# A graph network on one core: one-hot matrices moved to the scalar engine, and a node update as a wave

## The chip, the cores and the metric

The kernel runs on one core of a Trainium2 chip. The metric is the device time of one execution in microseconds (us). The core has five engines with queues of their own, which wait for each other through semaphores: TensorE (PE in the profile; its weight loads PEld), VectorE (DVE), the scalar engine (ACT), GpSimd (POOL), and SyncE (SP), which only issues transfers (DMAs).

## The reference, cut to what matters

Four graph layers run one after another on 6250 nodes with 16 features and 206250 edges sorted by destination. Nothing in the computation is changed; what follows is what the passes of the kernel compute.

```
A0, N0  m = silu(einsum(x[col], edge_attr_8, W_msg_tp)) @ W_msg_lin ; agg = segment_sum(m)
        u = silu(einsum(x, agg, W_upd_tp)) @ W_upd_lin ; x = norm(x + u)
1 to 6  six graph convolutions: h @ W, times dinv, segment sums over the edges
7       sums of x[src] * edge_weight with a running maximum over each destination's segment
        (and, beside it, relu(edge_attr_13 @ f1 + b), stored for 8 and 9)
8, 9    message e = reshape(edge_net(e), 16 x 16) @ h[src e] ; segment sum ; GRU step
```

Passes 7, 8 and 9 each go over all edges, gather a row of 16 numbers per edge, and add a result per edge into its destination's column.

## The kernel before, in words

Edges stand in 1632 tiles of 128 (one edge per partition); a batch is HT = 8 tiles, and there are NB = 204 batches, in a hardware loop of 51 turns with SL = 4 batches each. Every counter of a pass is a semaphore with a fixed number of steps per batch (`VPER` for VectorE, `TPER` for TensorE, `APER` for the scalar engine), and `at(k, step)` is its value when that step of batch k is done. h = k mod 2 picks one of two buffers.

**Cells (GpSimd, during A0 and after).** GpSimd scatters one cell per edge into the adjacency table `adj` with indirect DMAs (L591), eight per batch, and copies pairs out of `acc` (L582) ahead of each batch. It is behind A0 and ends later than A0 does. Passes 1 to 6 read `adj` in blocks (L533), and their first load waits for all cells.

**N0.** After A0 the node update runs over 13 chunks of 512 nodes, one chunk after the other, 25 steps each, each step waiting for the one before on another engine (L749 to L764 on TensorE). Its steps write `stage`, `tst`, `acc` and `arena`. `acc` still holds the pairs that GpSimd copies, so from the seventh chunk on VectorE waits for the last copy. The block loads of pass 1 wait for N0's last step. The later updates N1 to N5 are already waves: four chunks (SETS) are in flight, each with its own banks and semaphore, and the engines walk an order of (chunk, step) written out by `wave`.

**Passes 7 to 9.** GpSimd gathers: eight indirect DMAs per batch (L562), each 128 rows by indices in SBUF (`idx`), into one of four buffers `G`. It waits once per two batches, for VectorE to be done (step `USED`) with the batches that had these buffers, and for the indices. VectorE, per batch:

- loads eight destination starts into registers (`load_firsts`, L1207, L1208), and makes the one-hot (L1199): for 8 tiles, iota of 128 against `rel`, the edge's place within its tile's window, in bf16;
- subtracts for the lowest bf16 piece of the last batch's message (`lower`, L1224); a message is split in three bf16 pieces, the first two copied by the scalar engine (high L1177 or L1157, middle L1179 or L1164);
- waits for the gather and makes the message: in pass 7 L1666, then L1669, L1671 and a scan (L1676); in passes 8 and 9 four multiplies (L1711) of TensorE's products (L916, from `rT`) by the gathered rows, and a reduction (L1716);
- adds eight windows into `acc` at the registers' columns (L1215), and takes the remainder after the high piece (`remains`, L1229).

TensorE multiplies the pieces by the one-hot (`windows`, L625, eight products of a batch) once the lower piece is there. In pass 8 and 9 it does so for batch k - 1 behind the products of batch k. SyncE loads `rT` for a batch two batches on, when the remainder is taken (L484).

## Time and profile before

| | |
|---|---|
| median of 3 runs | 12295.55 us (12293.52 to 12299.69) |
| the profiled execution | 12296.19 us |
| its span, first to last instruction | 12294.4 us |
| mean granted TensorE clock | 0.667 of full speed |
| busy: TensorE, VectorE, scalar engine, GpSimd | 74%, 65%, 16%, 57% |

The stages in the span: set-up and A0 to 2630 us, N0 to 3140, passes 1 to 6 with their updates to 5430, pass 7 to 7800, pass 8 to 10030, pass 9 to the end. The profile names each group of instructions by line, engine, operation and tiles (out<-in), with the time it was busy and the idle time of its engine just before it, which is put down to what came last ("issue" where nothing that the profile shows was waited for). The windows view gives for a stretch of the span its length, the busy us and number of instructions of PE, PEld, DVE, ACT and POOL, and then the granted clock as a share of 2.4 GHz, the DMA share and GB/s.

### The profile page before, as it was taken

The numbers are of one execution on the slowest core, as the hardware profiler recorded it, in microseconds if no ns is written. First come the engines' busy times: TensorE is split into PE (matmuls) and PEld (weight loads), VectorE is DVE, ScalarE is ACT, GpSimd is POOL, SyncE is SP. The second block draws the span as 40 slices with busy tenths as digits, with TensorE's granted clock in tenths as the row PEclk, the third lists the DMA queues.
The fourth block names the chain that finished last, engine by engine and source line by source line (L and its number), as shares of the span: only waits on it lengthen the run. The fifth ranks groups of instructions, "written<-read, shape, count | busy, mean of one in ns | idle before, by whom it ended". The sixth has DMA issues, their size and how long they took to land.

```text
span 12294.4 us, 191432 instructions
## 1 busy us (share of the span) xinstructions
PE 9044.8 (74%) x51270; PEld 6037.7 (49%) x51270; DVE 7967.3 (65%) x14983; ACT 1906.5 (16%) x6193; POOL 7005.9 (57%) x6789
## 2 busy tenths in 40 slices
PE   0499999974578998756666666677777767777776
PEld 0366666641367787532222222355555545555554
DVE  1599999962122222237777777688888868888887
ACT  2454333321000100001111111000000000000000
POOL 0588788873000000027777777577777757777775
PEclk9999999975578898755555555555555555555555
DMA  7633444310887887861111111111111111111111
GB/s 253 213 104 104 118 107 109 108 50 0 258 261 242 261 287 237 278 205 33 34 34 34 34 33 34 26 19 19 19 19 19 19 20 19 19 19 19 19 19 20
DMA packets 1340598, 1146.05 MB, mean 93 GB/s; under 512 B 329039, under 2 KB 1225504, under 8 KB 1340190
## 3 DMA queue, kind: packets, MB, share of 16 engines
q1 hardware_dynamic: 1108690, 1064.47, 28.4%
q0 software_dynamic: 210560, 44.35, 4.8%
q10 hardware_dynamic: 21186, 34.95, 0.9%
q8 instruction: 116, 1.90, 0.1%
q14 instruction: 46, 0.38, 0.0%
HBM read 994.01 MB, written 144.62 MB: 93 GB/s over the span
## 4 chain that ended last, share of the span: by engine, by line
DVE 34%; PE 16%; issue 10%; DMA 7%; DVEq 7%; POOL 1%; ACT 1%; SPq 0%; POOLq 0%; ACTq 0%
DVE acc L1215 10%; DVE arena L1711 8%; DVE msg L1716 7%; DMA arena<-adj 7%; PE ps L797 7%; DVE arena L1676 4%; PE ps L876 3%; DVEq L1207 2%; PE ps L809 2%; DVEq L1215 2%; PE ps L625 2%; DVE threes L1224 1%; DVE sc L1229 1%; DVEq L1208 1%; POOL arena L562 1%
## 5 line engine op out<-in xcount | busy, mean ns | idle before, releaser
L562 POOL DMA_INDIRECT arena<-tab,idx x4896 | 4984.4, 1018 | 4315.2 <-DMA idx<-in_src_p 2619.6
L916 PE MATMUL ps<-w_w2b,arena 33*128 33x256 f32 x6528 | 2931.4, 640 | 39.7 <-DMA arena<-rT 21.9
L916 PEld LDWEIGHTS ps<-w_w2b,arena 33*128 33x128 f32 x6528 | 2106.9, 330 | 652.4 <-issue 119.0
L591 POOL DMA_INDIRECT adj<-pairs x1632 | 1865.1, 1143 | 488.1 <-issue 417.6
L625 PE MATMUL ps<-arena,threes 128*48 128x128 bf16 x4912 | 625.2, 308 | 1680.8 <-DVE threes L1224 1680.8
L1215 DVE TENSOR_TENSOR acc<-acc,ps 48x128 f32 x4920 | 1377.9, 280 | 652.5 <-PE ps L625 3.9
L625 PEld LDWEIGHTS ps<-arena,threes 128*48 128x48 bf16 x4912 | 486.9, 151 | 2287.6 <-issue 2287.6
L797 PE MATMUL ps<-arena 128*128 128x192 bf16 (+1 forms) x18816 | 1374.1, 235 | 297.7 <-DMA arena<-adj 288.6
L797 PEld LDWEIGHTS ps<-arena 128*128 128x128 bf16 x18816 | 1290.0, 104 | 394.2 <-issue 389.0
L1711 DVE TENSOR_TENSOR arena<-ps,arena 128x512 f32<-128x512 f32 x1632 | 1010.7, 681 | 26.5 <-DMA arena<-tab,idx 26.5
L1716 DVE TENSOR_REDUCE msg<-arena 128x128 f32<-128x2048 f32 x408 | 932.7, 2286 | 14.1
L994 ACT ACTIVATE wide<-ps,not_all 128x128 bf16<-128x128 f32 x1632 | 572.8, 377 | 1238.7 <-PE ps L693 1238.5
L1199 DVE TENSOR_TENSOR arena<-w_iota,rel 128x1024 bf16<-128x1024 f32 x408 | 500.9, 1228 | 385.6 <-PE ps L916 265.1
L1378 DVE TENSOR_TENSOR arena<-hot_a,threes 128x1024 bf16<-128x1024 bf16 x612 | 745.8, 1219 | 0.0
L1526 DVE TENSOR_REDUCE wide<-ps 128x128 f32<-128x384 f32 (+1 forms) x192 | 79.0, 453 | 986.3 <-PE ps L797 986.3
L1676 DVE TENSOR_TENSOR_SCAN arena<-arena,carry,ps 16x1024 f32<-16x1024 f32 x204 | 476.1, 2334 | 215.4 <-PE ps L876 215.4
L1177 ACT ACTIVATE threes<-msg 128x128 bf16<-128x128 f32 x408 | 126.2, 309 | 2832.8 <-DVE msg L1716 2826.0
L687 PE MATMUL ps<-arena 128*128 128x128 f32 x3264 | 402.7, 277 | 186.8 <-DMA arena<-tab 174.1
L1507 DVE TENSOR_TENSOR acc<-acc,ps 64x128 f32 (+1 forms) x408 | 113.7, 279 | 614.1 <-PE ps L774 572.8
L687 PEld LDWEIGHTS ps<-arena 128*128 128x128 f32 x3264 | 396.3, 194 | 201.7 <-DVEq L1372 174.7
L729 PE MATMUL ps<-acc,arena 128*128 128x392 bf16 x2448 | 422.6, 329 | 0.0
L887 PEld LDWEIGHTS ps<-w_ident,arena 16*128 16x128 f32 x1632 | 171.2, 195 | 504.8 <-issue 504.8
(241 smaller groups left out, 10059.7 us busy)
## 6 DMA issues: line engine op xcount, KB each, us to landing
arena<-adj SPq DMA_DIRECT2D x672, 896.0 KB, 7.9
arena<-rels SPq DMA_DIRECT2D x204, 512.0 KB
arena<-tab SPq DMA_DIRECT2D x1632, 64.0 KB
adj<-zero SPq DMA_DIRECT2D x49, 2048.0 KB, 20.7
arena<-tab,idx POOLq DMA_INDIRECT x4896, 2.4
arena<-rT SPq DMA_DIRECT2D x408, 128.0 KB
adj<-pairs POOLq DMA_INDIRECT x1632
rT<-spare ACTq DMA_DIRECT2D x204, 128.0 KB
```

The costliest lines, as they stand in the source:

```text
L562: pool.indirect_dma_start(G[b][:, u, 0:FEAT[PHASES[p]]], None, TABLE[PHASES[p]], bass.IndirectOffsetOnAxis(ap=idx[b // 2][:, b % 2 * HT + ...
L591: pool.indirect_dma_start(adj_cells, bass.IndirectOffsetOnAxis(ap=pairs[h][:, u, 0:1], axis=0), pairs16[h][:, u, 2:3], None).then_inc(cell ...
L625: last = mm(ps[0:48, 2 * h + u // 4, (u % 4) * P:(u % 4 + 1) * P], threes[h][:, u, :, :].rearrange("p k f -> p (k f)"), hot[h][:, u, :], s ...
L687: last = mm(ps[:, 2 + 2 * h + u // 4, (u % 4) * P:(u % 4 + 1) * P], hotT[h][:, u * P:(u + 1) * P], nodes0[h][:, u, :], start=True, stop=True)
L797: last = mm(ps[:, 2 * par + u // 2, u % 2 * W:(u % 2 + 1) * W], ring[i][:, s, u * P:(u + 1) * P], rows[:, j * SC + s, :, :].rearrange("p k ...
L916: last = mm(ps[:, 4 + q, (u % 2) * 256:(u % 2 + 1) * 256], row[h][0:33, u * P:(u + 1) * P], w["w2b"][:, :], start=True, stop=True)
L994: act_fn(junk[u % 2], ps[:, 6 + u // 4, (u % 4) * P:(u % 4 + 1) * P], ACT.Relu, bias=not_all[:, :], accum_out=equals[h][:, u:u + 1]).then_ ...
L1215: tt(dst[0:F, ds(v, P)], dst[0:F, ds(v, P)], window(u), ALU.add).then_inc(vec[p].sem, 1)
L1378: tt(placed[h][:, i, :, :, :], hot_a[:, :, :].unsqueeze(3).to_broadcast([P, HT, A8, 16]), threes[h][:, :, i, :].unsqueeze(2).to_broadcast( ...
L1676: nc.vector.tensor_tensor_scan(wk[0:16, HE:], wk[0:16, 0:HE], ps[0:16, 4:6, :].rearrange("p q n -> p (q n)"), carry[:, 0:1], ALU.add, ALU. ...
L1711: tt(wk[:, q * 512:(q + 1) * 512].rearrange("p (u o i) -> p u o i", u=2, i=16), ps[:, 4 + q, :].rearrange("p (u o i) -> p u o i", u=2, i=1 ...
L1716: nc.vector.tensor_reduce(msg[h][:, :, :].rearrange("p u o -> p (u o)"), wk[:, :].rearrange("p (x i) -> p x i", i=16), AX, ALU.add).then_i ...
```

## The change

Two parts.

In passes 7, 8 and 9 VectorE no longer makes one-hots. The scalar engine does, a batch ahead: after the middle piece of batch k it writes, for each of 8 tiles of batch k + 1, the square of (rel - iota) into `far2` (Square with scale -1 and a bias per partition), and then Relu(1 - 2 x square) of all 1024 columns into `hot`, after TensorE's windows that last read this buffer. `rel` and `rel_last` are padded by a batch, since the last turn makes a one-hot that nobody reads. TensorE's windows wait for the scalar engine's count too. VectorE's step numbers go down by one. Its register load is behind L1671 in pass 7; in passes 8 and 9 it is done for two batches at a time, 16 registers, in every even batch.

N0 becomes a wave like N1 to N5, of 26 steps, four chunks in flight, with buffers of their own in `arena` (`a_0` to `t_0`), the 256-row product in two halves, and no copies of x. The column of `acc` that each chunk kept is no longer written by a step: two multiplies of x and dinv after the wave do it, the first for columns 0 to 3263, the second, after all cells have landed, for the rest. The block loads of pass 1 wait for the cells and the wave. At the start, two memsets become one and two are new.

```diff
+        far2 = arena[:, 7 * HE:8 * HE].rearrange("p (u n) -> p u n", u=HT)
...
-        K = dict(A0=3, N0=25)
-        WAVES = dict(N1=11, N2=12, N3=21, N4=12, N5=11)
+        K = dict(A0=3)
+        WAVES = dict(N0=26, N1=11, N2=12, N3=21, N4=12, N5=11)
...
-        USED = [None] + [None] * 6 + [3, 6, 6]
-
-        VPER = [18] + [7] * 6 + [8 + HT] * 3
+        USED = [None] + [None] * 6 + [2, 5, 5]
+
+        VPER = [18] + [7] * 6 + [7 + HT] * 3
         TPER = [2 + HT] + [NCH + 1] * 6 + [5, 5, 5]
-        APER = [3 + HT, 1, 1, 1, 1, 1, 1, 4, 2, 2]
+        APER = [3 + HT, 1, 1, 1, 1, 1, 1, 6, 4, 4]
         LOADS = [0, 0, 0, 0, 0, 0, 0, 4, 1, 1]
...
-        LOWER = 2
-        MSG, CHANGED, RESET, SCAN, CARRY = range(3, 8)
-        MUL = [3, 4, 5, 6]
-        MESSAGES = 7
-        END0 = 8
+        LOWER = 1
+        MSG, CHANGED, RESET, SCAN, CARRY = range(2, 7)
+        MUL = [2, 3, 4, 5]
+        MESSAGES = 6
+        END0 = 7
         REMAINS = END0 + HT
         WT = [1, 2, 3, 4]
         WINDOWS8 = 5
...
                 if p == 1:
-                    before = node[PHASES[p]]
-                    sp.wait_ge(before.sem, before.at(NC - 1, before.per))
+                    nodes_done(sp, 1)
...
             def windows(p, k, h):
 
+                pe.wait_ge(scl[p].sem, scl[p].at(k - 1, APER[p]))
                 pe.wait_ge(vec[p].sem, vec[p].at(k + 1, LOWER))
...
+            for c, step in wave("N0"):
+                i, x = c % SETS, xT[:, c * CH:(c + 1) * CH]
+                if step == 1:
+                    wave_wait(pe, "N0", c, 1)
+                    for a8 in range(A8):
+                        last = mm(ps[0:16, 2 * i, :].rearrange("p (b a) -> p a b", a=A8)[:, a8, :],
+                                  lin8[:, a8 * 16:(a8 + 1) * 16], agg[:, c * (CH // A8):(c + 1) * (CH // A8)],
+                                  start=True, stop=True)
+                    last.then_inc(wave_sem[i], 1)
+                elif step in (3, 6):
+                    wave_wait(pe, "N0", c, step)
+                    half = slice(0, P) if step == 3 else slice(P, 2 * P)
+                    mm(ps[:, 2 * i, :], w["rep_i"][:, half], x, start=True, stop=True)
+                    mm(ps[:, 2 * i + 1, :], w["rep_h"][:, half], a_0[i][0:16, :], start=True, stop=True
+                       ).then_inc(wave_sem[i], 1)
+                elif step == 9:
+                    wave_wait(pe, "N0", c, 9)
+                    mm(ps[0:16, 2 * i, :], w["upd_tp"][:, 0:16], x_0[i], start=True, stop=False)
+                    mm(ps[0:16, 2 * i, :], w["upd_tp"][:, 16:32], y_0[i], start=False, stop=True).then_inc(wave_sem[i], 1)
+                elif step == 11:
...
+            for c, step in wave("N0"):
+                i = c % SETS
+                if step in (2, 4, 7, 10, 18, 23, 25):
+                    wave_wait(act, "N0", c, step)
+                low, high = ps[:, 2 * i, :], ps[:, 2 * i + 1, :]
+                p_w, rows = piece(16)[:, c * 4:c * 4 + 4, :, :], low[:, 0:64].rearrange("p (j f) -> p j f", j=4)
+                if step == 2:
+                    act_fn(a_0[i][0:16, :], low[0:16, :], ACT.Copy, scale=0.25).then_inc(wave_sem[i], 1)
+                elif step == 4:
+                    act_fn(x_0[i], low, ACT.Copy).then_inc(wave_sem[i], 1)
...
-            open_pass(act, scl[7], 7)
+            def squares(p, k, h, r):
+
+                for u in range(HT):
+                    last = act_fn(far2[:, u, :], w["iota"][:, :], ACT.Square, scale=-1.0, bias=r[:, ds(k * HT + u, 1)])
+                last.then_inc(scl[p].sem, 1)
+
+            def one_hot(p, k, h):
+
+                act.wait_ge(scl[p].sem, scl[p].at(k - 1, APER[p] - 1))
+                act_fn(hot[h][:, :, :], far2[:, :, :], ACT.Relu, scale=-2.0, bias=unit[:, :]).then_inc(scl[p].sem, 1)
+
+            def open_one_hots(p, r):
+
+                stage_done(act, PHASES[p])
+                act.sem_inc(scl[p].sem, SL * APER[p] - 2)
+                squares(p, 0, 0, r)
+                one_hot(p, 0, 0)
+
+            open_one_hots(7, rel_last)
...
+                    act.wait_ge(scl[7].sem, scl[7].at(k - 1, APER[7]))
+                    squares(7, k + 1, 1 - h, rel_last)
+                    act.wait_ge(ten[7].sem, ten[7].at(k - 1, WINDOWS7))
+                    one_hot(7, k + 1, 1 - h)
...
+                        act.wait_ge(scl[p].sem, scl[p].at(k - 1, APER[p]))
+                        squares(p, k + 1, 1 - h, rel)
+                        act.wait_ge(ten[p].sem, ten[p].at(k, WINDOWS8))
+                        one_hot(p, k + 1, 1 - h)
...
-            def one_hot(p, k, h, r):
-
-                dve.wait_ge(ten[p].sem, ten[p].at(k - 2, TPER[p]))
-                tt(hot[h][:, :, :], w["iota"][:, :].unsqueeze(1).to_broadcast([P, HT, P]),
-                   r[:, ds(k * HT, HT)].unsqueeze(2).to_broadcast([P, HT, P]), ALU.is_equal
-                   ).then_inc(vec[p].sem, 1)
-
-            first_node = [dve.alloc_register(f"first_node{u}") for u in range(HT)]
-
-            def load_firsts(k):
-
-                dve.load(first_node, base[0:1, ds(k * HT + HT, HT)])
-                return [dve.snap(r, min_val=0, max_val=N) for r in first_node]
+            first_node = [dve.alloc_register(f"first_node{u}") for u in range(2 * HT)]
+
+            def load_firsts(k, n=HT):
+
+                dve.load(first_node[0:n], base[0:1, ds(k * HT + HT, n)])
+                return [dve.snap(r, min_val=0, max_val=N) for r in first_node[0:n]]
...
-            with dve.Fori(0, 2 * T // CH) as c:
-                update_nodes(c)
-            dve.wait_ge(pairs_in, NB)
-            with dve.Fori(2 * T // CH, NC) as c:
-                update_nodes(c)
+            for c, step in wave("N0"):
+                i, x = c % SETS, xT[:, c * CH:(c + 1) * CH]
+                if step in (5, 8, 12, 13, 15, 16, 19, 20, 21, 24, 26):
...
+                if step == 5:
+                    tt(x_0[i], x_0[i], high, ALU.mult).then_inc(wave_sem[i], 1)
+                elif step == 8:
+                    tt(y_0[i], y_0[i], high, ALU.mult).then_inc(wave_sem[i], 1)
...
+            nodes_done(dve, 1)
+            tt(acc[0:16, 0:2 * T], xT[:, 0:2 * T], dinv[0:16, 0:2 * T], ALU.mult).then_inc(sums_open, 1)
+            for h in range(2):
+                dve.wait_ge(celled[h], 16 * HT * NB // 2)
+            tt(acc[0:16, 2 * T:], xT[:, 2 * T:], dinv[0:16, 2 * T:], ALU.mult).then_inc(sums_open, 1)
+            dve.wait_ge(sums_open, 2)
...
-                    at = load_firsts(k - 1)
-                    one_hot(7, k, h, rel_last)
                     lower(7, k - 1, 1 - h)
...
 
+                    at = load_firsts(k - 1)
                     dve.wait_ge(v.sem, v.at(k, RESET))
...
-                        at = load_firsts(k - 1)
-                        one_hot(p, k, h, rel)
+                        if h == 0:
+                            at = load_firsts(k - 1, 2 * HT)
                         lower(p, k - 1, 1 - h)
```

## Rows read from the trace of the kernel before

**Rows 1.** The page, parts 1, 4 and 5: totals, chain by line, costly groups.
```profile
PE 9044.8 (74%) x51270; PEld 6037.7 (49%) x51270; DVE 7967.3 (65%) x14983; ACT 1906.5 (16%) x6193; POOL 7005.9 (57%) x6789
...
DVE acc L1215 10%; DVE arena L1711 8%; DVE msg L1716 7%; DMA arena<-adj 7%; PE ps L797 7%; DVE arena L1676 4%; PE ps L876 3%; DVEq L1207 2%; PE ps L809 2%; DVEq L1215 2%; PE ps L625 2%; DVE threes L1224 1%; DVE sc L1229 1%; DVEq L1208 1%; POOL arena L562 1%
...
L1716 DVE TENSOR_REDUCE msg<-arena 128x128 f32<-128x2048 f32 x408 | 932.7, 2286 | 14.1
```

**Rows 2.** One line's instructions, passes 7, 8, 9: ns min/median/max, first and last start.
```profile
L1666 DVE TENSOR_TENSOR msg<-arena,col x204: 278/286/293, 5451.7 to 7780.5; 128x128 f32<-128x128 f32 x102
...
L1711 DVE TENSOR_TENSOR arena<-ps,arena x816: 673/681/692, 7850.8 to 10003.9; 128x512 f32<-128x512 f32 x164
...
L1711 DVE TENSOR_TENSOR arena<-ps,arena x816: 679/681/692, 10078.6 to 12224.0; 128x512 f32<-128x512 f32 x164
```

**Rows 3.** The gathers of pass 9: durations, starts, idle time before them, landing.
```profile
L562 POOL DMA_INDIRECT arena<-tab,idx x1632: 940/944/1920, 10067.3 to 12217.8; - x182
...
  issue: 497.1, 1631
...
DMA to landing us min/median/max: 2.1/2.4/3.6
```

**Rows 4.** Windows of N0, of the N3 wave and of pass 9.
```profile
2631.00:3140.00 509.00, 234.09 (x494) 69.04 (x494) 129.44 (x158) 93.17 (x117) 221.28 (x250) 0.52 0.01 0
4224.00:4347.00 123.00, 104.95 (x156) 15.79 (x156) 63.72 (x116) 51.44 (x91) 0.00 (x0) 0.51 0.09 29
10200.00:12140.00 1940.00, 1498.12 (x4410) 1093.70 (x4410) 1570.49 (x2942) 113.52 (x367) 1492.02 (x1471) 0.50 0.13 19
```

**Rows 5.** Timeline of pass 8, one batch's turn: start us, duration us, engine, line.
```profile
9014.17 0.28 DVE L1229 TENSOR_TENSOR sc<-msg,threes 128x128 f32<-128x128 f32 x1
9014.48 0.31 ACT L1179 ACTIVATE threes<-sc 128x128 bf16<-128x128 f32 x1 [3.09 <-DVE sc L1229]
9014.62 0.32 SPq L484 DMA_DIRECT2D arena<-rT  x1
...
9015.21 1.22 DVE L1199 TENSOR_TENSOR arena<-w_iota,rel 128x1024 bf16<-128x1024 f32 x1 [0.76 <-PE ps L916]
9015.91 1.34 POOL L562 DMA_INDIRECT arena<-tab,idx  x1 [0.30 <-issue]
9016.35 0.28 DVE L1224 TENSOR_TENSOR threes<-sc,threes 128x128 bf16<-128x128 f32 x1
9016.55 1.28 DVE L1711 TENSOR_TENSOR arena<-ps,arena 128x512 f32<-128x512 f32 x2
...
9016.78 1.02 PE L625 MATMUL ps<-arena,threes 128*48 128x128 bf16 x8 [2.25 <-DVE threes L1224]
```

**Rows 6.** Register loads on VectorE's queue, passes 8 and 9.
```profile
L1207 DVEq TENSOR_LOAD <-base x402: 593/598/811, 7901.4 to 12198.9; - x134
```

**Rows 7.** Groups of the scalar engine in N0: busy us, mean ns.
```profile
L958 ACT ACT_TABLE_LOAD x39 | 50.0, 1283 | 1.2
...
L958 ACT ACTIVATE arena<-ps 128x1024 f32<-128x1024 f32 x13 | 13.3, 1023 | 170.1 <-PE ps L755 170.1
```

**Rows 8.** Timeline of pass 7, VectorE alone.
```profile
6515.10 0.28 DVE L1229 TENSOR_TENSOR sc<-ps,threes 128x128 f32<-128x128 f32 x1
...
6517.28 0.29 DVE L1224 TENSOR_TENSOR threes<-sc,threes 128x128 bf16<-128x128 f32 x1
6517.48 0.28 DVE L1666 TENSOR_TENSOR msg<-arena,col 128x128 f32<-128x128 f32 x1
6517.69 1.21 DVE L1669 TENSOR_TENSOR arena<-arena 16x1024 f32<-16x1024 int32 x1
```

**Rows 9.** Timeline: end of the scatters, first block load, first product of pass 1.
```profile
2918.13 0.95 POOL L591 DMA_INDIRECT adj<-pairs  x1 [0.30 <-issue]
...
3140.17 26.20 SPq L533 DMA_DIRECT2D arena<-adj  x10
...
3146.55 1.28 PE L797 MATMUL ps<-arena 128*128 128x48 bf16 x28 [5.94 <-DMA arena<-adj]
```

More of the change, by code:

```diff
@@ L743, in _, with product @@
             mm(ps[:, 7, 0:Q // P], first[:, :], node_q[:, :], start=True, stop=True).then_inc(positions, 1)
[L744 removed]
+            def product(name, c, step, F, out, lhsT, rhs):
+                wave_wait(pe, name, c, step)
+                mm(ps[0:F, 2 * (c % SETS) + out, :], lhsT, rhs, start=True, stop=True).then_inc(wave_sem[c % SETS], 1)
             pe.wait_ge(agg_in, 2)
[L746 to L764 removed]
@@ new lines, in _ @@
+            for c, step in wave("N0"):
[18 more added lines that the diff above has]
+                elif step == 11:
+                    product("N0", c, 11, 16, 1, w["upd_lin"][:, :], b_0[i][0:16, :])
+                elif step == 14:
+                    product("N0", c, 14, 16, 0, w["mean16"][:, :], b_0[i][0:16, :])
+                elif step == 17:
+                    product("N0", c, 17, 16, 1, w["mean16"][:, :], a_0[i][0:16, :])
+                elif step == 22:
+                    wave_wait(pe, "N0", c, 22)
+                    for j in range(4):
+                        last = nc.tensor.transpose(ps[:, 2 * i, j * 16:(j + 1) * 16], g_0[i][0:16, j * P:(j + 1) * P],
+                                                   w["ident"][0:16, 0:16])
+                    last.then_inc(wave_sem[i], 1)
@@ L805, in sum_pass @@
                     ten[p + 1].open(pe)
-            def product(name, c, step, F, out, lhsT, rhs):
-                wave_wait(pe, name, c, step)
-                mm(ps[0:F, 2 * (c % SETS) + out, :], lhsT, rhs, start=True, stop=True).then_inc(wave_sem[c % SETS], 1)
             def wave_rows(name, c, step, F, out):
@@ L1170, in _ @@
             for p in (8, 9):
[L1171 removed]
+                open_one_hots(p, rel)
                 with act.Fori(0, IT) as it:
@@ L1283, in split_rest @@
                    ).then_inc(n.sem, 1)
-            for half in range(2):
-                nc.vector.memset(zero[:, half * CH // 2:(half + 1) * CH // 2], 0.0).then_inc(ready, 1)
+            nc.vector.memset(zero[:, :], 0.0).then_inc(ready, 1)
+            nc.vector.memset(rel_last[:, T:], 0.0).then_inc(ready, 1)
             nc.vector.memset(lin8[:, :], 0.0).then_inc(ready, 1)
@@ L1720, in _ @@
                         dve.wait_ge(ten[p].sem, ten[p].at(k, WINDOWS8))
-                        add_windows(p, k, at, acc, 48, END0, range(HT), half_window(1 - h, 48))
+                        add_windows(p, k, at[h * HT:(h + 1) * HT], acc, 48, END0, range(HT), half_window(1 - h, 48))
                         remains(p, k, h, msg[h][:, :, :])
```

96 lines of the change are left out of this document (46 added, 50 removed).

## The prediction

> **What bounds the kernel now.** I read the engine totals and the chain first. VectorE is busy 65% of the span, GpSimd 57%, and the chain is led by VectorE's adds, multiplies and reductions [rows 1]. That suggests a kernel bound by VectorE, where each instruction taken off it is time won. The views by pass say otherwise.
>
> The last three passes have 204 batches each. In pass 9, VectorE's first multiply starts at 10078.6 and its last, the fourth of its batch (three times some 0.6 behind the first), at 12224.0: (12222.2 - 10078.6) / 203 = 10.56 us a batch; in pass 8 it is 10.60, in pass 7 11.47 [rows 2]. Now GpSimd: 1632 gathers in pass 9, median 0.944 us, and the idle time before them, 497.1 us in 1631 gaps, is put down to nothing but issue: 0.305 each [rows 3]. In a stretch of that pass GpSimd's mean is 1492.02 / 1471 = 1.014 [rows 4], and 8 x (1.014 + 0.305) = 10.55: a whole batch. GpSimd never waits; both engines fill the batch.
>
> The timeline of one batch shows what couples them [rows 5]. The one-hot (L1199) runs 9015.21 to 9016.43. The gather that starts inside it, at 9015.91, takes 1.34 instead of 0.94 and ends at 9017.25, 0.82 after the one-hot. A median gather ends 0.82 after a point 0.13 from its start, so I read: a gather reads its indices there and is held until the one-hot ends. Multiplies (one input in PSUM) hold none. GpSimd's own pace is 8 x (0.944 + 0.305) = 9.99 us a batch; the rest is the one-hot's hold, once a batch.
>
> **One-hots to the scalar engine (VectorE side).** Call R the start of the remainder (L1229). Today: R at 9014.17, register load, one-hot at 9015.21, lower piece (L1224) at 9016.35, multiply at 9016.55, so 2.38 from R [rows 5]. The load (0.6 [rows 6], and what uses it) fills the 1.04 before the one-hot. Without one-hot the lower piece waits for the scalar copy of the middle piece (L1179, 9014.48 to 9014.79, hidden today): it starts at R + 0.66 and the multiply at R + 0.86. Every second batch of passes 8 and 9 still loads registers there, 16 now: no row has 16, bounds are one load's 0.6 and two loads' 1.2; I take 0.9, lower piece at R + 1.3. VectorE's batch becomes 10.60 - 2.38 + 0.86 = 9.1, or 9.7: mean 9.4; with the dear load 9.55.
>
> **The gathers' side.** 9.99 is above 9.4, so GpSimd sets passes 8 and 9, and of the 1.2 us that VectorE loses only 0.6 is won. The last batch's first multiply comes 203 x 9.99 = 2028 after the first batch's. Pass 8: 7850.8 + 2028 = 9878.8 against 10003.9 - 1.8 = 10002.1: 123.3. Pass 9: 12106.6 against 12222.2: 115.6. Sum 238.9 [rows 2, 3]; the lower piece (two inputs in SBUF, 0.28) may hold a few gathers, so 235, range 200 to 240.
>
> [...]
>
> **Scalar engine.** Added per batch: eight squares of 128x128 and a Relu of 128x1024. The nearest rows are L1179's 0.31 (128x128) and 1.02 (L958, 128x1024) [rows 5, 7]: 8 x 0.31 + 1.02 = 3.5. As upper bound I double the square, since each takes its bias from a computed address: 6.0. They start after the middle copy, R + 0.62, and end at R + 4.1 (6.6). Queued behind is the next high copy, possible at R + 0.86 + 2.5 + 2.3 = R + 5.7 [rows 1, 5], needed only by the next remainder three microseconds on. At 3.5 nothing is late, at 6.0 the slack takes it. TensorE reads a one-hot a batch later. If Square is not in the loaded table, two loads of 1.28 [rows 7] are added: 6.1, hidden too. [...]
>
> **TensorE** is busy 1498.12 in 1940 us, 8.2 a batch [rows 4]. It fits 9.99. Its rT load, issued at R + 0.45 (9014.62 [rows 5]), would be needed 1.5 earlier than today; 2.4 us of landing, the gathers' own [rows 3], gives R + 2.8; with the 7.2 of products (8.2 less the windows' 1.0 [rows 5]) they end at R + 10.0, and the last multiply wants them at R + 0.86 + 1.9 + 9.99: hidden.
>
> **Pass 7.** R to lower piece is 2.18 today (6515.10 to 6517.28) [rows 8]. It becomes 0.74 (the scalar copy stands behind a Relu there); from the lower piece on, TensorE's windows and transposes set the scan as now; the register load moves under L1671. VectorE: 11.47 - 1.44 = 10.0. GpSimd: 9.99 plus the hold of L1669, which stays: two SBUF inputs, 1.21 us, nearly the 1.25 between two gathers' starts, so some gather nearly always meets it. Once VectorE follows the landing, its place is fixed: with E the end of the eighth gather and D its landing time, L1669, 0.21 behind the message multiply [rows 8], runs from E + D + 0.26 to E + D + 1.47; gathers read at E + 1.68 and E + 2.93. D of 1.45 to 1.68 costs 0 to 0.2, D of 1.9 costs 0.4, D below 1.42 a full 1.2. Landing from start is 2.4 [rows 3] (D 1.4 to 1.5), longer when SyncE's four loads go out at the same time, as they would here; I take D = 1.9: 10.4 a batch, (11.47 - 10.4) x 203 = 217. Bounds: 10.05 (288) and 11.18 (59).
>
> **N0.** Today the last scatter of cells starts at 2918.13 (landed about 2920.3); the first block load is issued at 3140.17, and the first product of pass 1 is at 3146.55 [rows 9]. As a wave, N0 is bound by TensorE: 234.1 us of products [rows 4]. The N3 wave kept TensorE busy 104.95 of 123 us at a granted clock of 0.51 [rows 4], 85%: 234.1 / 0.85 = 275, so N0 ends at 2906, under the scatters, which then gate the loads: first product at 2920.3 + 6.4 = 2926.7, 220 earlier. The two new multiplies into acc (3264 and 3392 columns; at L1711's 0.64 for 512 [rows 5], 4.2 each) run before and within those 6.4. If the clock rose the wave would be shorter and nothing gained. Two-input instructions may hold scatters: 216. At 70% it ends at 2965 and 173 is left.
>
> **Sum.** 216 + 217 + 235 = 668 off the profiled 12296.2 (span 12294.4; median of the runs 12295.55, the same): 11628.
>
> **Rivals.**
> A. VectorE alone sets the pace, as the chain says: (10.6 - 9.4) x 408 = 490, pass 7 298, N0 216: 11292. Against it: gathers cannot go below 9.99. Chance 0.05.
> B. Gathers are not freed: another cause makes them 1.014 in the mean. Passes 8 and 9 stay near 10.55 and win nothing; pass 7 at about 10.8 wins 136, N0 216: 11944. Against it: each long gather overlaps a one-hot. 0.08.
> C. Pass 7 settles in the full hold, 11.18: 11786. 0.12.
> D. Slower: a scalar batch longer than today's 10.6, from (10.6 - 1.6) / 8 = 1.1 us a square (small instructions with an address and bias from registers could be dear). At 1.3, 12.0 a batch: 408 x 1.45 + 203 x 1.9 - 216 = 761 slower, 13057. Against it: 0.31 in each such row. 0.03, with 0.01 of it near no change.
> My forecast has 0.72.
>
> **Range.** Best bounds: 220 + 288 + 240 = 748, 11548. C with nothing else is 11786. 11540 to 11800 leaves out A, B, D and a bit of C with a late wave. A change within 0.2% (25 us) can't be told from none: faster 0.97, same 0.01, slower 0.02.
>
> **What would show it.** Passes 8 and 9: gather mean back at 0.944 to 0.95, no gather over 1.3, the multiply released by the landing, batch 9.99. Pass 7: gathers still over 1.0 beside L1669, message multiply waiting for the gather. N0: last step before 2930, first block load at 2920 to 2925. Wrong if the gathers stay long, if the multiply waits for TensorE or the lower piece for the scalar engine past R + 1, or if the wave passes 2960.

## The result, and the profile after

| | before | after |
|---|---|---|
| median time, us | 12297.62 (4 runs, 12293.52 to 12306.68) | 11517.97 (4 runs, 11513.64 to 11525.68) |
| profiled execution, us | 12296.19 | 11525.68 |

The ratio is 0.9366, 95% interval 0.935 to 0.9382: 780 us saved, where 668 were forecast, and a time 22 us below the low end of the range. The direction was right, and so were the mechanisms of the three terms; the sum lacked a fourth term.

Page of the changed kernel, parts 1, 4 and 5 (against [rows 1]):

```profile
PE 8973.8 (78%) x51270; PEld 6020.0 (52%) x51270; DVE 7298.7 (63%) x14361; ACT 4035.9 (35%) x11725; POOL 6700.9 (58%) x6789
...
POOL arena L569 31%; PE ps L820 8%; DMA arena<-adj 5%; DVE msg L1779 3%; PE ps L754 2%; DVE arena L1774 2%; DMA arena<-tab,idx 2%; PE ps L935 2%; DVE acc L1266 1%; PE ps L797 1%; PE ps L633 1%; ACT x_all L1106 0%; SPq L455 0%; DMA arena<-rT 0%; DVE x_all L1606 0%
...
L1184 ACT ACTIVATE arena<-w_iota,rel 128x128 f32<-128x128 f32 x3280 | 998.1, 386 | 0.2
...
L1190 ACT ACTIVATE arena<-arena,unit 128x1024 bf16<-128x1024 f32 x615 | 706.0, 1148 | 20.0
```

The chain, led by VectorE's adds, multiplies and reductions before, is now led by GpSimd's gathers (L569, 31%). The views by line say the same of passes 8 and 9. First the multiply of both passes and what its engine waited for, in the kernel before:

```profile
L1711 DVE TENSOR_TENSOR arena<-ps,arena x1632: 673/681/692, 7850.8 to 12224.0; 128x512 f32<-128x512 f32 x182
...
  DMA arena<-tab,idx: 26.5, 2
```

The same after the change, pass by pass, and then the gathers of pass 9 (against [rows 2, 3]):

```profile
L1774 DVE TENSOR_TENSOR arena<-ps,arena x816: 673/680/693, 7317.5 to 9349.3; 128x512 f32<-128x512 f32 x164
...
L1774 DVE TENSOR_TENSOR arena<-ps,arena x816: 673/680/693, 9423.2 to 11453.1; 128x512 f32<-128x512 f32 x164
...
  DMA arena<-tab,idx: 186.6, 219
```

```profile
L569 POOL DMA_INDIRECT arena<-tab,idx x1632: 940/944/1063, 9412.0 to 11448.0; - x182
its engine sat idle before it (us, times) until:
  issue: 481.8, 1581
...
DMA to landing us min/median/max: 2.2/2.4/3.3
```

The longest gather of pass 9 is 1.06 us (1.92 before). A batch of pass 8 is (9349.3 - 1.8 - 7317.5) / 203 = 10.00 us, of pass 9 9.99, forecast 9.99. In 219 of the 408 batches VectorE's multiply now waits for the landing of a gather, 0.46 us a batch in the mean; before, it did so twice, once at the start of each pass.

N0's end, and the first products of pass 1 (timeline; against [rows 9]):

```profile
2928.69 0.95 POOL L598 DMA_INDIRECT adj<-pairs  x1 [0.30 <-issue]
...
2931.06 3.68 DVE L1556 TENSOR_TENSOR acc<-x_all,dinv 16x3392 f32<-16x3392 f32 x1 [45.43 <-DMA adj<-pairs]
2931.37 17.52 SPq L540 DMA_DIRECT2D arena<-adj  x8
...
2936.94 1.28 PE L820 MATMUL ps<-arena 128*128 128x48 bf16 x28 [1.64 <-DMA arena<-adj]
```

The wave was done early: VectorE had waited 45 us for the scatters before the second of its two multiplies. The last scatter starts 10.6 us later than before, the first product 209.6 earlier.

One line remains, the one that the prediction never asked for: the products of the six passes with sums, in the kernel before and after, from the first of pass 1 to the last of pass 6.

```profile
L797 PE MATMUL ps<-arena x18816: 182/246/368, 3146.6 to 5396.9; 128*128 128x192 bf16 x132, 128*128 128x48 bf16 x67
```

```profile
L820 PE MATMUL ps<-arena x18816: 182/246/368, 2936.9 to 5109.9; 128*128 128x192 bf16 x132, 128*128 128x48 bf16 x67
```

2250.3 us became 2173.0, though no instruction of these passes was changed. The spans' difference of 770.5 us is made up so (the 0.2 us that the rows lack are rounding and the step from the last product to the first gather):

| stretch | saved, us | forecast |
|---|---|---|
| up to the first product of pass 1 | 209.6 | 216 |
| passes 1 to 6 and their updates | 77.3 | none |
| first gather of pass 7 (5440.3; 5153.2) to first multiply of pass 8 | 246.2 | 217 |
| from there to the end | 237.2 | 235 |

### The profile page after: what moved, and what is told of

It is laid out like the page before. It is cut to its first block, busy times and chain, and to the rows that moved or that the text cites. A ratio compares the mean times of both kernels' runs of the same rounds, so it can differ in the third digit from the quotient of the medians.

```text
span 11523.9 us, 201355 instructions
## 1 busy us (share of the span) xinstructions
PE 8973.8 (78%) x51270; PEld 6020.0 (52%) x51270; DVE 7298.7 (63%) x14361; ACT 4035.9 (35%) x11725; POOL 6700.9 (58%) x6789
## 4 chain that ended last, share of the span: by engine, by line
POOL 31%; PE 14%; issue 12%; DMA 8%; DVE 7%; DVEq 1%; ACT 1%; SPq 1%; POOLq 0%; ACTq 0%
POOL arena L569 31%; PE ps L820 8%; DMA arena<-adj 5%; DVE msg L1779 3%; PE ps L754 2%; DVE arena L1774 2%; DMA arena<-tab,idx 2%; PE ps L935 2%; DVE acc L1266 1%; PE ps L797 1%; PE ps L633 1%; ACT x_all L1106 0%; SPq L455 0%; DMA arena<-rT 0%; DVE x_all L1606 0%
## 5 line engine op out<-in xcount | busy, mean ns | idle before, releaser
L569 POOL DMA_INDIRECT arena<-tab,idx x4896 | 4675.6, 955 | 3843.8 <-DMA idx<-in_src_p 2290.4
L820 PE MATMUL ps<-arena 128*128 128x192 bf16 (+1 forms) x18816 | 1341.5, 234 | 229.9 <-DMA arena<-adj 214.4
L1184 ACT ACTIVATE arena<-w_iota,rel 128x128 f32<-128x128 f32 x3280 | 998.1, 386 | 0.2
L1190 ACT ACTIVATE arena<-arena,unit 128x1024 bf16<-128x1024 f32 x615 | 706.0, 1148 | 20.0
L1233 ACT ACTIVATE threes<-sc 128x128 bf16<-128x128 f32 x408 | 126.2, 309 | 1295.3 <-DVE sc L1280 1295.3
L1275 DVE TENSOR_TENSOR threes<-sc,threes 128x128 bf16<-128x128 f32 x615 | 181.7, 295 | 588.1 <-issue 334.8
```

The costliest lines, as they stand in the source:

```text
L569: pool.indirect_dma_start(G[b][:, u, 0:FEAT[PHASES[p]]], None, TABLE[PHASES[p]], bass.IndirectOffsetOnAxis(ap=idx[b // 2][:, b % 2 * HT + ...
L820: last = mm(ps[:, 2 * par + u // 2, u % 2 * W:(u % 2 + 1) * W], ring[i][:, s, u * P:(u + 1) * P], rows[:, j * SC + s, :, :].rearrange("p k ...
L1184: last = act_fn(far2[:, u, :], w["iota"][:, :], ACT.Square, scale=-1.0, bias=r[:, ds(k * HT + u, 1)])
L1190: act_fn(hot[h][:, :, :], far2[:, :, :], ACT.Relu, scale=-2.0, bias=unit[:, :]).then_inc(scl[p].sem, 1)
```

## Experiments

Two things must be known to read them. First, of 18 runs only three (chunks_half, chunks_fit, arena_128), all on one chip, were made where the kernel before takes its 12297 us. On the four other chips it took 14771 to 15108. There single register instructions of VectorE, SyncE and, after the change, the scalar engine take up to 1.4 us instead of 0.05, and the work behind them starts later; I call this late streams. The register instruction ahead of each add, in the kernel before where it takes 12297 us:

```profile
L1215 DVEq FUSED_REGOPS  x4920: 46/46/46, 5456.7 to 12235.2; - x197
```

and with late streams, in the kernel before with a pad, with what the adds waited for:

```profile
L1216 DVEq FUSED_REGOPS  x4920: 1/46/1423, 6066.5 to 14946.6; - x197
...
its engine sat idle before it (us, times) until:
  issue: 745.7, 408
```

That "issue" is time in which the adds waited for nothing that the profile shows; in the kernel before without late streams they have none of it. So the times of passes 7 to 9 say little about the change there. Passes 1 to 6 hardly depend on it: the changed kernel's 2173.0 us was 2176.2 with late streams, and 2170.3 to 2183.5 in the four runs that edit passes 7 to 9 alone (mults_sbuf, its two repeats, no_compare). Differences under some 10 us are therefore not read. Second, the measure for passes 1 to 6 is always the one above, first to last product.

### The arena's place

The change adds tiles ahead of the arena, which receives the block loads in packets of 1024 bytes: eight columns to rel_last, and unit, 36 bytes per partition as declared. The arena's place is named below by the declared bytes that stand ahead of it and don't in the kernel before: 0 there, 36 after the change. The address at which it then begins stands in no trace; where an expectation counts a move otherwise (64 for the change's tiles in hots_part, 128 in arena_128), that is the expectation's own count, which no run shows.

```diff
+        pad = sb("pad", [P, 9])     # before_pad36; [P, 7] in after_pad28, [P, 1] in before_pad4
         eps = sb("eps", [P, 1])
```

> The kernel before with one unused tile of 36 bytes per partition ahead of eps and of the arena; no instruction changes. Passes 1 to 6, which the prediction took as unchanged, gave back about 77 us of the change's 780 (the profiled executions: 2293.8 us from the first product of pass 1 to the first gather before, 2216.3 after). Theory A (the change moved the arena by 36 bytes per partition, and the 1024-byte packets of the block loads then take 46 ns instead of 46 to 60): the packets take 46 ns here too, passes 1, 3, 4 and 6 become about 19, 8, 8 and 19 us shorter and passes 2 and 5 about 12, and the run is about 78 us faster, near 12220. Theory B (the loops of the passes stand elsewhere in the instruction stream, and other loops have to be fetched over and over): nothing moves here, 12297 within 0.2%, and passes 2 and 5 stay the long ones of the middle four.

Measured: ratio 0.9939 (0.9917 to 0.9961), 15008 against 15098 us; first to last product 3861.9 to 6006.8, 2144.9 us: 105 shorter than before by an unused tile, where 78 were expected. Theory A holds.

> The changed kernel with one unused tile of 28 bytes per partition, so that the arena stands 64 bytes behind its place in the kernel before, at the same remainder by 64. Theory A (the arena's place sets the packets' time): the 1024-byte packets of the block loads go back to 46 to 60 ns, and about 78 us of the 780 are lost: 11596. Theory B (the place of the loops in the instruction stream): 11518 within 0.2%.

Measured: 0.9821 (0.9801 to 0.984) and 2270.8 us, 98 longer than the changed kernel. With 64 declared bytes ahead of it the arena is at a slow place again. The control is the changed kernel as it is:

> The changed kernel as it is, as the control of the two that follow, and against its version with 28 more bytes per partition, which gave 0.9821 of the kernel before. If the arena's place is worth the same 0.6% here, this one gives about 0.976 on a chip like that of the first four runs, and 0.937 on one like that of the kernel's own runs.

Measured: 0.9799 (0.9774 to 0.9824), 2176.2 us. The stretch shows A; the intervals of the two ratios overlap, and they come from two chips.

> The kernel before with one unused tile of 4 bytes per partition ahead of eps, instead of the 36 of the first pad; no instruction changes. The 36 bytes took about 90 us off. [...]

Measured: ratio 1.0 (0.9985 to 1.0015), 2254.0 us. Four bytes do nothing (2250.3 without them); the pad of 36 gave 2144.9.

> The changed kernel with three small tiles moved from behind the arena to ahead of it and one of 4 bytes added, so that the arena begins 128 bytes later per partition. [...]

Measured, with 12299 for the kernel before: 11606.37 us (11599.45 to 11610.59), 0.9436, and 2257.3 us. The four tiles declare 16 bytes, 52 with the change's 36: a slow place. This is the one run that shows the arena's place in the time of the whole kernel: 88 us over the changed kernel's 11518, with intervals of the ratios that don't meet. The packets themselves, DMA view of 2960 to 3020 in this kernel and in the changed one:

```profile
GB/s 350 348 348 349 350 350 351 349 348 349 350 346 349 348 350 348 349 348 348 350 348 347 355 343 350 348 350 357 339 349 348 348 349 350 348 347 355 335 331 276
```

```profile
GB/s 386 388 384 380 380 385 388 384 386 387 384 378 384 385 386 379 386 386 386 377 384 385 386 359 383 386 385 387 386 386 386 389 353 359 280 83 1 11 68 251
```

With its queues full, the core moves 349 GB/s into one arena and 386 into the other. By packet: in every run with the arena at 36, 97 to 98% take 46 or 47 ns; at the four other places, 0, 4, 52 and 64, 37 to 40% do, and the mean is 51. The fast place was one in all runs, and what sets it apart from the other four wasn't shown.

### The place of the loops

Within passes 1 to 6 some got longer. Of the kernel before, passes 2 and 3, and of the changed one, passes 2 and 3 again (the products; then, from the DMA view of each pass, the queue of instruction fetches: packets, MB, share). Before:

```profile
L797 PE MATMUL ps<-arena x3136: 242/246/364, 3517.6 to 3841.9; 128*128 128x192 bf16 x196
...
L797 PE MATMUL ps<-arena x3136: 242/246/364, 3922.9 to 4219.3; 128*128 128x192 bf16 x196
```

```profile
q8 instruction: 35, 0.57, 0.6%
...
q8 instruction: 7, 0.11, 0.1%
```

After:

```profile
L820 PE MATMUL ps<-arena x3132: 242/246/368, 3289.6 to 3579.0; 128*128 128x192 bf16 x196
...
L820 PE MATMUL ps<-arena x3136: 242/246/368, 3660.0 to 3973.3; 128*128 128x192 bf16 x196
```

```profile
q8 instruction: 7, 0.11, 0.2%
...
q8 instruction: 35, 0.57, 0.5%
```

324.3 and 296.4 us became 289.4 (290.0 with the first four products, which the window leaves out) and 313.3, and the fetches changed sides with the time (a window holds one or two fetches more than its pass). The traces also show the size of a fetch in instructions. A packet is 16384 bytes; in the passes 2 to 5 that got six of them, before and after, TensorE's stream had 256 to 265 instruction records from one to the next in the mean, and a round of the loop has 1696 (6783 in the four). And they show where a loop begins beside the fetches: in the passes 2 to 5 with six fetches, in these two kernels, a fetch came 89 to 104 records ahead of the first product; in those with 34 none came in the 40 us ahead of it, and the first came 10 to 37 records behind it. So TensorE's stream got fillers:

```diff
+                for _ in range(FILL[p]):      # half: 120 for p = 1; fit: 36, 34, 16, 118 for p = 1, 3, 4, 5
+                    pe.sem_inc(filler, 1)
                 nodes_done(pe, p)
```

> The changed kernel with 120 increments of an unused semaphore on TensorE's queue ahead of pass 1. TensorE's instruction stream is read in packets of 16 KB, 256 instructions of 64 bytes; the loop of one of the passes 1 to 6 is 1700 instructions, 6.64 packets. Counted in the compiled streams, the loops that begin in the first third of a packet (passes 3, 4 and 6 before; 2 and 5 after the change) are those whose trace has 6 such packets, and those that begin later (2 and 5 before; 1, 3 and 4 after) have 33 and last 22 to 26 us longer. Theory B1 (a loop that lies in 8 packets is read again in every round, one in 7 is not): the 120 put the loops back where the kernel before has them: pass 1 falls from 295 to about 273 us (the run with 36 bytes), 3 and 4 from 308 to 282, 6 from 271 to 263, passes 2 and 5 rise from 283 to about 307; the sum from 1746 to about 1715, 30 us off the changed kernel. Theory B2 (the fetches only go with long passes, something else sets them): the pattern stays, long passes 1, 3 and 4, and the time within 0.2%.

Measured: 11496.57 us (11495.05 to 11500.42), 0.9349 (0.9337 to 0.9362); passes 272, 312, 287, 289, 316 and 263 us (counted from first to last product of each, which is 1 to 5 more than the count in the expectation), 2147.6 in all against 2173.0. The fetches changed sides with the loops, and 120 instructions that do nothing made this stretch 25 us shorter: B1 holds. In the whole kernel that is 0.2%, and there the ratio's interval still meets that of the changed kernel (0.935 to 0.9382).

> The changed kernel with 36, 34, 16 and 118 such increments ahead of passes 1, 3, 4 and 5, so that every one of the six loops begins in the first third of a packet of 16 KB of TensorE's stream. Theory B1: no pass is read again, six fetches each; passes 1 to 6 at about 273, 282, 282, 282, 282 and 263 us, 1664 instead of 1746: 80 us less, 0.5 to 0.7% off the changed kernel and the fastest version so far. Theory B2: no change, or the increments' own time of 5 to 10 us more.

Measured: 11488.05 us (11483.96 to 11491.57), 0.9342 (0.9329 to 0.9355), 30 off instead of 80; first to last product 2134.8 us. Passes 1, 3, 4 and 6 as expected, 3, 4 and 5 with a fetch 4 to 17 records ahead of their first product. Two misses: pass 2 was read again (34 fetches, 314 us), with its first fetch 169 records behind its first product and none just ahead; and the 118 increments ahead of pass 5 stand bare, 18 us in which TensorE does nothing:

```profile
4465.41 0.80 PE L814 MATMUL ps<-arena,zero 128*128 128x384 bf16 x2 [18.02 <-issue]
```

The next version spreads them over the groups of the update ahead, where TensorE waits anyway:

```diff
+            first_step = dict(N1=2, N2=2, N3=4, N4=2, N5=4)
             def product(name, c, step, F, out, lhsT, rhs):
+                if step == first_step.get(name):
+                    fill(FILL[int(name[1])] * (c + 1) // NC - FILL[int(name[1])] * c // NC)
                 wave_wait(pe, name, c, step)
```

> The changed kernel with all six loops of passes 1 to 6 in the first quarter of a 16 KB packet of TensorE's stream (the sixth at 0.34, where it had 6 fetches in the last version): 100 increments ahead of pass 1, and 106, 122, 16 and 118 spread over the groups of the updates N1 to N4, each just ahead of a product for which TensorE waits anyway (an increment took 0.15 us; 8 or 9 of them against a wait of 1.1 to 1.4 us). Theory B1: six fetches in every pass; the passes at about 266, 282, 282, 281, 282 and 263 us, 1656 instead of 1744, with up to 10 us lost again in the updates: 11518 - 78 = 11440. If pass 2 is still read again, the place within the packet isn't the rule.

Measured, with 14773 for the kernel before: 14409.16 us, 0.9751 (0.9726 to 0.9777), 80 us below the changed kernel's 14488.97, which was measured where the kernel before took the same time (14771). First to last product 2102.0, and no pass is read again; in passes 2 to 5 a fetch came 32 to 53 records ahead of the first product. Once more:

> The version with all six loops early in a packet, once more. In its first run every pass had 6 fetches and passes 1 to 6 took 272, 284, 284, 285, 285 and 264 us, 1674 in sum (1746 for the changed kernel on such a chip), and the kernel 0.9751 of the one before against 0.9799 for the changed kernel. Where no engine's stream is late (the kernel before at 12297): 11518 - 70 + up to 10 for the increments = 11448 to 11458. On the other kind of chip: 0.975 again.

Measured: late streams again (15108 for the kernel before), 0.9717 (0.969 to 0.9743; 0.975 was expected), 2105.3 us. Its pass 2, 289.9 us with 6 fetches:

```profile
L832 PE MATMUL ps<-arena x3136: 242/246/364, 3995.4 to 4285.3; 128*128 128x192 bf16 x196
```

```profile
q8 instruction: 6, 0.10, 0.1%
```

It is the fastest version by these stretches; its time where the kernel before takes 12297 wasn't measured.

### The two parts by themselves

n0_part applies the lines on N0 alone, hots_part the rest.

> The kernel before with N0's wave alone; arena, one-hots and registers as before. Up to the first product of pass 1 the profiled executions differ by 210 us. Theory A (arena's place, which stays here): 12297 - 210 = 12087. Theory B (the unrolled wave moves the loops of passes 1 to 6 in the instruction stream): 12297 - 210 - 77 = 12010, with passes 3 and 4 the long ones of the middle four, as in the changed kernel. A mixture: the long passes change places, but the sum of passes 1 to 6 stays at 2294 us.

> The kernel before with the part on passes 7 to 9 alone: one-hots on the scalar engine a batch ahead, registers for two batches, and the tiles that they bring (so the arena is moved by 36 bytes here too); N0 stays the loop of 25 steps. The time after N0 accounts for 246 (pass 7) and 238 (passes 8 and 9) of the saving in the profiled executions. Theory A (arena's place) adds the 77 of passes 1 to 6: 12297 - 484 - 77 = 11736. Theory B (place in the instruction stream, which the unrolled wave of N0 moves): 12297 - 484 = 11813, and passes 2 and 5 stay the long ones of the middle four, as before.

Measured: 0.9885 (0.9865 to 0.9904) with 2273.2 us, and 0.9872 (0.9852 to 0.9892) with 2149.1. The mixture: the wave makes passes 1 to 6 longer, by 23 us, the other part makes them 101 shorter. Both had late streams, so what the parts are worth in the whole kernel stayed open. The same kernels again:

> N0's wave alone, the kernel of the first four runs once more, on a chip whose time for the kernel before is hoped to be 12297 rather than 15098. First product of pass 1 at 2937 instead of 3147 (210 us), and passes 1 to 6 slower by 20 to 28 us, as the loops come to lie as after the change (three read again instead of two) while the arena stays at its slow place: 12297 - 210 + 25 = 12112. If passes 1 to 6 come out faster, the account of the 77 us is wrong.

> The one-hots on the scalar engine and the registers for two batches, N0 as before; the arena moves by 64 bytes to its fast place. Passes 7 to 9 take 484 us less, passes 1 to 6 about 100 to 105 less (arena's place, the loops stay where they were): 12297 - 484 - 103 = 11710. Together with N0's part: 187 + 587 = 774 against 780 measured.

> The part on passes 7 to 9 once more. Where no engine's stream is late: 12297 - 484 (passes 7 to 9) - 103 (arena's place in passes 1 to 6) = 11710. On the other kind of chip 0.993 again, with pass 7 some 250 us longer and passes 8 and 9 some 125 us shorter each than in the kernel before.

Measured, with late streams all three times: n0_part 0.9873 (0.9843 to 0.9904), 2273.3 us; hots_part 0.9932 (0.9906 to 0.9959), 2150.4 us; hots_part_2 0.9865 (0.9837 to 0.9894), 2157.1 us. The stretch repeats; the ratio doesn't: one kernel gave 0.9872, 0.9932 and 0.9865 on three chips, further apart than the intervals. What each part is worth where the kernel before takes 12297 us was not measured as a whole; only the stretches of the changed kernel's trace say it. With late streams the one-hot part costs pass 7 some 250 us (first to last gather 2896.9 us in the kernel before with the 4-byte pad, 3147.7 in the changed kernel) and wins 129 and 137 in passes 8 and 9. The scalar engine's register instructions, 46 ns each in the changed kernel's own trace, are late there too: up to 1.4 us. The cause of the 250 wasn't pursued.

### What holds a gather

```diff
                             tt(wk[:, q * 512:(q + 1) * 512]...,
-                               ps[:, 4 + q, :]...
+                               zero[:, :]...                                # mults_sbuf
-                    tt(wk[0:16, 0:HE], row[h][0:16, :].bitcast(i32), prev[h][0:16, :], ALU.not_equal)
+                    ts(wk[0:16, 0:HE], row[h][0:16, :].bitcast(i32), 0, None, ALU.not_equal)    # no_compare
```

> The changed kernel; in passes 8 and 9 the four multiplies of a batch take their first operand from a tile of zeros in SBUF instead of PSUM, so both operands lie in SBUF (leaves out: the products' values; sizes and order stay). Theory A (a gather whose descriptors are being made waits for the end of a VectorE operation with two SBUF operands): the multiplies last 4 x 0.68 = 2.7 us a batch, in which two gathers start and each is held for half a multiply on average or longer: 0.7 us a batch or more, passes 8 and 9 at least 285 us longer in the profile, and gathers of up to 1.6 us. Theory B (only particular operations hold a gather, not where the operands lie): gathers stay at 0.94 to 1.06 us and the time within 0.2% of the changed kernel.

Measured: 0.9773 (0.9742 to 0.9805), no slower than the changed kernel, since with late streams gathers don't set the pace. The holds are there, though. Gathers of pass 8 in the control (after_again) and in mults_sbuf, and one instance of each kind (timelines of the changed kernel and of mults_sbuf):

```profile
L569 POOL DMA_INDIRECT arena<-tab,idx x1624: 938/945/997, 9046.9 to 11674.4; - x181
```

```profile
L569 POOL DMA_INDIRECT arena<-tab,idx x1624: 938/945/1472, 9039.2 to 11645.6; - x181
```

```profile
8007.32 2.48 DVE L1774 TENSOR_TENSOR arena<-ps,arena 128x512 f32<-128x512 f32 x4 [0.68 <-DMA arena<-tab,idx]
8008.54 0.94 POOL L569 DMA_INDIRECT arena<-tab,idx  x1 [0.30 <-issue]
```

```profile
9808.86 2.49 DVE L1774 TENSOR_TENSOR arena<-zero,arena 128x512 f32<-128x512 f32 x4
9809.70 1.26 POOL L569 DMA_INDIRECT arena<-tab,idx  x1 [0.30 <-issue]
```

In mults_sbuf the second of the four multiplies ends about 0.3 us behind the gather's read point, and that gather takes 0.3 longer. Summed over the records of passes 8 and 9: of 329 gathers whose read point (0.13 us behind their start) lies in such a multiply, 228 are long and end 0.82 behind its end. The other 101 read within its first 0.17 us, and all that read later are held. With the operand in PSUM none is held, of 418 in the control. Where the operand lies decides: theory A in kind, with a size that these executions can't give.

> The changed kernel; in pass 7 the comparison of the edge's node with the one before it (1.2 us, two SBUF operands) is a comparison with the constant 0, one SBUF operand (leaves out: where the segments of the maximum begin). Theory A (this comparison is what still holds one gather a batch in pass 7): the gathers of pass 7 fall from a mean of 0.976 to 0.944 us, the batch from 10.26 to about 9.99 us, pass 7 is about 55 us shorter. Theory B (the rest of pass 7's batch comes from VectorE's own chain): pass 7 within 10 us of the changed kernel's.

Measured: 0.9821 (0.9796 to 0.9846), and pass 7 no shorter (13 us longer than the control's from first to last gather, both with late streams). A fell as put: the hold didn't go, it moved to the operation behind (timeline of pass 7, this kernel):

```profile
6504.84 0.68 DVE L1731 TENSOR_SCALAR arena<-arena 16x1024 f32<-16x1024 int32 x1
6505.55 0.68 DVE L1733 TENSOR_SCALAR arena<-arena 16x1024 f32<-16x1024 f32 x1
6505.95 1.11 POOL L569 DMA_INDIRECT arena<-tab,idx  x1 [0.30 <-issue]
```

By the records 170 of 170 gathers that read inside L1733 (a tensor_scalar, one operand, in SBUF) end 0.82 behind it, and 30 of 38 inside L1731, all but those in its first 0.14 us. In the changed kernel 11 gathers read in the first 0.1 us of L1733, and none was held by it. The scan, the adds and the multiplies (an operand in PSUM) and the reduction (SBUF alone) hold none or next to none.

> The changed kernel with the multiplies of passes 8 and 9 reading zeros in SBUF instead of PSUM, once more where no engine's stream is late. In the first run 228 of the 329 gathers whose read point (126 ns behind their start) fell into such a multiply ended 818 ns behind its end, against 0 of 422 with the operand in PSUM, and were held for a third of a microsecond on average. Theory A (an elementwise VectorE operation with every operand in SBUF holds the gathers): about two gathers a batch start in a multiply, 0.3 to 0.7 us a batch more, 120 to 285 us over the changed kernel's 11518. Theory B (VectorE's gain of some tenths, since it no longer waits for products, outweighs it): within 0.2% of 11518.

> The multiplies on zeros in SBUF once more. Where no engine's stream is late: theory A (elementwise operations with all operands in SBUF hold the gathers) 120 to 285 us over 11518; theory B within 0.2% of it. On the other kind of chip, where the gathers wait for the late stream anyway, 0.976 again and held time of some 35 us a pass.

Measured: 0.976 (0.973 to 0.979) and 0.9723 (0.9695 to 0.975); late streams both times, and holds again, 28 to 33 us a pass. What a hold costs in passes 8 and 9 where gathers set the pace stays open.

## Why the prediction was wrong, step by step

**What bounds the kernel, and passes 8 and 9: right.** Gathers had been held by the one-hot, 201 times in the 204 batches of pass 9 and 164 times in pass 8; freed, they set the pace at 9.99 us a batch. 237 us for 235. In pass 8 the holds came to 80 us of the 121 by which it got shorter. VectorE's own chain, which almost never waited for a gather, took 10.60 there, a little more than the gathers, which waited for it 12 times: the two were level, as the prediction says, and both had to get shorter. VectorE's side was mis-sized, and the margin hid it: the lower piece starts 0.65 behind R in batches without a load (0.66 forecast), but in those with the load of sixteen, where 1.3 was taken, 1.69 behind R in one half and 2.1 to 2.2 in the other (one of the first kind, timeline of pass 8, R and the lower piece). Since VectorE still waits 0.46 a batch for landings, its mean stays under 9.99.

```profile
8415.21 0.28 DVE L1280 TENSOR_TENSOR sc<-msg,threes 128x128 f32<-128x128 f32 x1
8416.90 0.29 DVE L1275 TENSOR_TENSOR threes<-sc,threes 128x128 bf16<-128x128 f32 x1 [1.41 <-issue]
```

**Scalar engine: right.** Eight squares are 386 ns each by the page of the profile but 2.45 us back to back, the Relu 1.15: 3.6 us a batch for a forecast of 3.5, with 6.0 as bound, and no table was loaded within the passes. Rival D had no ground.

**N0: right.** 209.6 for 216; the wave, at a granted clock of 0.61 (0.52 in [rows 4]), was done 45 us or more before the scatters, which gated the loads. The missing 6 are the later end of the scatters, 10.6 us where 4 were allowed: 4 of them stood before N0 began, and in the wave the scatters were held for some 5.

**Pass 7: right in kind, the hold mis-sized.** 246 for 217, within its bounds of 59 and 288. The batch is (7246.7 - 5164.6) / 203 = 10.26 us, not 10.4. The hold by the comparison is there (a gather in L1731's reach, changed kernel):

```profile
6006.75 1.21 DVE L1731 TENSOR_TENSOR arena<-arena 16x1024 f32<-16x1024 int32 x1
...
6007.76 1.05 POOL L569 DMA_INDIRECT arena<-tab,idx  x1 [0.30 <-issue]
```

but all holds of pass 7 come to 55 us over 204 batches by the records, 51 of them by this comparison: 0.27 a batch instead of 0.4, and 9.99 + 0.27 is the 10.26. That the sum came near is in part luck, for the picture of the hold's place was off: the message multiply waits for the landing in 51 of 204 batches, not in each, so its place to the gathers isn't fixed by the landing.

**Passes 1 to 6: the step that failed.** The sum is "216 + 217 + 235 = 668 off the profiled 12296.2": it has no term for the 2250 us between the first product of pass 1 and the last of pass 6, as nothing is edited there. The runs put two in its place (the 2147.6 is chunks_half, the changed kernel whose 120 increments put the loops back):

| first to last product, us | loops as before | loops as moved by N0's wave |
|---|---|---|
| arena at 0, 4, 52 or 64 | 2250.3, 2254.0 | 2273.2, 2273.3, 2270.8, 2257.3 |
| arena at 36 | 2144.9, 2149.1, 2150.4, 2157.1, 2147.6 | 2173.0, 2176.2 |

The new tiles put the arena at its fast place: about -100 (81 to 109 between the rows). N0's wave, unrolled, moves every later loop in TensorE's stream, so that three of them (1, 3 and 4) are read again instead of two (2 and 5): about +25 (16 to 31 between the columns; only arena_128's 2257.3 lies no more than 3 to 7 above the left one, and why wasn't found). Sum -77, as measured. With 668 + 77 and pass 7's 29 more, the forecast would have been 11522.

A trace of both stood there before the run: the diff adds tiles ahead of the arena, and in the trace before passes 2 and 5 are 27 us longer than 3 and 4 with the same work. From the second a term of some 27 us for each loop that changes sides could have been put. The sign of the whole could not: no row before showed that the arena's place matters, and the loops' places need the length of the stream.

Which loops are read again the expectations put down to the packets of 256 instructions that a loop lies in, eight against seven. The traces show the place of the fetches alone. In passes 2 to 5 of every trace the loops with a fetch 4 to 104 instruction records ahead of their first product had 6 fetches, and those whose first fetch came 8 to 45 behind it, and once 169, had 33 or 34. In passes 1 and 6 that doesn't decide: with the first fetch 245 records behind the first product, pass 1 had 15 in the kernel before and 6 with the pad of 36; with 93 and 95, pass 6 had 6 in after_pad28 and 16 in the changed kernel. Why a loop is kept or read again wasn't shown.

**Range.** Its low end came from the best bounds of the three terms, 748 us; 780 lay outside because the range, too, had only the three.

## What to carry to other kernels

An edit also moves what it doesn't touch: note where the big DMA destinations lie per partition, and how long each engine's stream and its loops are, before and after. Here the place of the buffer that takes the bandwidth-bound loads was worth 105 us of 12300, and TensorE's long loops beginning just behind a fetch of its instructions some 70, the latter by the stretch and not yet by the time of the whole kernel. And look for coupling before counting busy time: the one-hot cost VectorE 1.2 us a batch, but the batch fell by 0.6, down to the gathers' own pace, and even that only because the gathers that it held became free.

## What the runs showed of the hardware

- Packets of 1024 bytes into the arena took 46 or 47 ns nearly all (97 to 98%), 47.3 to 47.7 in the mean, with the arena where the change puts it (36 declared bytes ahead), and 51 in the mean with 0, 4, 52 or 64 ahead (386 against 349 GB/s for the core in the changed kernel and in arena_128).
- A loop of 1700 TensorE instructions took 21 to 30 us more over its four rounds where it was read again, with 33 or 34 packets of 16 KB instead of 6. In the passes 2 to 5 read once, before and after, its stream had 256 to 265 instruction records from one packet to the next in the mean.
- GpSimd's gathers, which read their indices in SBUF, were held by elementwise VectorE operations whose operands all lie in SBUF, tensor_tensor and tensor_scalar, until 0.82 to 0.84 us behind their end (192 of 198 gathers that read inside L1731 in the changed kernel, 170 of 170 inside L1733 in no_compare). Multiplies with one operand in PSUM held none (0 of 418 in after_again), and of 774 gathers that read inside the reduction of the changed kernel, which reads SBUF alone, 2 took over 0.96 us. Whether the read of the indices is held or what follows it, the records don't tell.
- An increment of a semaphore took TensorE 0.15 us, 118 of them 18 us.
- In 15 of the 18 runs single register instructions of VectorE, SyncE and, after the change, the scalar engine took 0.7 to 1.4 us instead of 0.05, at the same few places of a loop, and the kernel before took 14.8 to 15.1 ms; the changed kernel is then 2% faster instead of 6.3%. No run of one chip showed it and all runs of the four others did; since the runs of a chip were made together, chip and moment can't be told apart. Why wasn't found.
